# Factorization-machine kernel: the first layer's weights in a transfer of 16 rows, and chunk 0 with the remainder in one

## The reference

```python
x_reg = input_data @ W_lin.T + b_lin                       # 12500 -> 1
emb = input_data @ factors                                 # 12500 -> 16
sum_squared = jnp.square(emb.sum(axis=1))
squared_sum = (jnp.square(input_data) @ jnp.square(factors)).sum(axis=1)
h = jax.nn.relu(emb @ W1.T + b1)                           # 16 -> 128
h = jax.nn.relu(h @ W2.T + b2)                             # 128 -> 64
dnn_out = h @ W3.T + b3                                    # 64 -> 1
x = x_reg + 0.5 * (sum_squared - squared_sum)[:, None] + dnn_out
x = 0.5 + jax.nn.sigmoid(x) * 5.0
```

## Time and profile before

| | |
|---|---|
| median of 3 runs | 133.77 us (133.70 to 133.78) |
| profiled execution | 133.86 us, span 132.0 us |
| TensorE busy | 107.0 us, 81% of the span |
| ScalarE, VectorE, GpSimd busy | 61.4, 52.6, 17.8 us |
| moved by DMA | 52.36 MB, mean 397 GB/s |
| mean granted clock of TensorE | 0.948 |
| chain that ended last | DMA 52%, PE 42%, SyncE's queue 2% |

### The profile page before, as it was taken

One profiled execution on the slowest core, in us unless ns is written; L12 is line 12 of the kernel. 1 busy time (PEld: TensorE's weight loads), 2 busy tenths in 40 slices (PEclk: granted clock), 3 DMA queues, 4 the chain that ended last, 5 costly groups with the idle time before them and its releaser, 6 DMA issues.

```text
span 132.0 us, 2605 instructions
## 1 busy us (share of the span) xinstructions
PE 107.0 (81%) x1123; PEld 34.3 (26%) x1123; DVE 52.6 (40%) x51; ACT 61.4 (47%) x52; POOL 17.8 (14%) x48
## 2 busy tenths in 40 slices
PE   6089569539999749969659979999569997999992
PEld 4012112012222112212112233322022222334881
DVE  0391063037036046045055016564075352576571
ACT  4030067039039049049058046867078472465851
POOL 3015000200046200110200110164200400000000
PEclk9999999965899977999986999999999999999999
DMA  3999899899989999998999999899899999999700
GB/s 115 397 528 427 377 477 452 367 447 477 427 367 477 432 397 437 477 417 387 467 447 397 427 477 417 382 467 437 382 427 432 437 410 422 416 399 413 306 23 1
DMA packets 3345, 52.36 MB, mean 397 GB/s; under 512 B 388, under 2 KB 520, under 8 KB 1544
## 3 DMA queue, kind: packets, MB, share of 16 engines
q1 hardware_dynamic: 3336, 52.23, 93.1%
HBM read 52.22 MB, written 0.00 MB: 396 GB/s over the span
## 4 chain that ended last, share of the span: by engine, by line
DMA 52%; PE 42%; SPq 2%; DVE 1%; issue 1%; ACT 1%
PE p_lin L506 37%; DMA xr<-in_x_pairs 36%; DMA xr<-in_x_end 16%; PE p_h L601 2%; PE p_sq L506 2%; PE p_tot L506 1%; PE p_h L632 1%; SPq L273 1%; DVE h L454 0%; DVE h L449 0%; PE p_tot L614 0%; SPq L267 0%; SPq L266 0%; SPq L265 0%; ACT lin L341 0%
## 5 line engine op out<-in xcount | busy, mean ns | idle before, releaser
L327 ACT ACTIVATE sq<-xr 128x2560 f32<-128x2560 f32 x20 | 45.8, 2331 | 46.6 <-DMA xr<-in_x_pairs 43.7
L427 DVE TENSOR_TENSOR sq<-xr 128x1536 f32<-128x1536 f32 x20 | 34.6, 1765 | 53.4 <-DMA xr<-in_x_pairs 48.8
L506 PE MATMUL p_lin<-xr,wr 128*17 128x512 f32 x320 | 42.3, 673 | 15.6 <-DMA xr<-in_x_pairs 15.6
L506 PE MATMUL p_lin<-sq,wz 128*18 128x512 f32 x320 | 36.5, 592 | 0.0
L506 PEld LDWEIGHTS p_lin<-xr,wr 128*17 128x17 f32 x320 | 9.6, 107 | 46.5 <-issue 39.7
L307 POOL COPY wr<-hd 128x136 f32 (+1 forms) x20 | 9.9, 495 | 77.6 <-PE p_lin L506 77.6
L506 PEld LDWEIGHTS p_lin<-sq,wz 128*18 128x18 f32 x320 | 9.8, 98 | 24.8 <-issue 24.7
L506 PE MATMUL p_lin<-xr,hd 128*17 128x352 f32 (+1 forms) x128 | 10.1, 380 | 1.3 <-DMA xr<-in_x_end 1.3
L437 DVE TENSOR_TENSOR sq<-xr 128x1408 f32<-128x1408 f32 (+3 forms) x6 | 6.6, 1134 | 6.2 <-DMA xr<-in_x_end 6.2
L337 ACT ACTIVATE sq<-xr 128x1408 f32<-128x1408 f32 (+3 forms) x6 | 5.7, 982 | 6.4 <-DMA xr<-in_x_end 6.4
L308 POOL COPY wz<-s_all 128x8 f32 (+1 forms) x20 | 7.0, 350 | 0.0
(11 more groups left out here) (52 smaller groups left out, 39.7 us busy)
## 6 DMA issues: line engine op xcount, KB each, us to landing
xr<-in_x_pairs SPq DMA_DIRECT2D x9, 4096.0 KB, 22.0
xr<-in_x_groups SPq DMA_DIRECT2D x2, 2048.0 KB, 17.7
xr<-in_x_end SPq DMA_DIRECT2D x1, 2112.0 KB, 17.2
xr<-in_x_end SPq DMA_DIRECT2D x3, 640.0 KB, 18.7
xr<-in_x_end SPq DMA_DIRECT2D x1, 1760.0 KB, 21.1
xr<-in_x_end SPq DMA_DIRECT2D x1, 1056.0 KB, 16.3
hd<-in_head SPq DMA_DIRECT2D x1, 952.0 KB, 4.8
xr<-in_x_end SPq DMA_DIRECT2D x1, 704.0 KB, 17.6
```

Source lines behind the costliest of these rows:

```text
L327: nc.scalar.activation(sq[:, ring(s), BY_DVE:CHUNKS, :], xr[:, s, BY_DVE:CHUNKS, :], ACT.Square).then_inc(act_squared, 1)
L427: nc.vector.tensor_tensor(sq[:, ring(s), 0:BY_DVE, :], xr[:, s, 0:BY_DVE, :], xr[:, s, 0:BY_DVE, :], ALU.mult).then_inc(dve_squared, 1)
L506: return nc.tensor.matmul(out, lhsT, rhs, start=False, stop=False, skip_group_check=True)
```

## The change

The first layer's weights leave the head: its rows have 1776 columns instead of 1904. They come in a transfer of their own, `w1_once` into the tile `w1_sel`: 16 rows of 256 columns, of which the first 128 are the weights, and the other 128 four identity matrices of 16 x 16, at columns 0, 32, 64 and 96, with zeros between them. At the end of its first stage TensorE multiplies the one by the other into the bank `p_h1[0]`, which gives the weights in four places with zeros in the other rows, and VectorE copies them from PSUM into the tile `w1`, which `first_layer` now reads. Chunk 0 and the remainder lie side by side in one tile `x_one` and in one array, and come in one transfer with one semaphore. Other functions are unchanged.

```diff
-C_W1 = 0
-C_W2 = C_W1 + H1
+C_W2 = 0
 C_B1 = C_W2 + H2
...
-def fm_kernel(nc, head, x_first, x_rest, x_pairs, x_groups, x_end, out):
+def fm_kernel(nc, head, w1_once, x_first, x_pairs, x_groups, x_end, out):
...
-        xf = sb("xf", [P, B])
-        xl = sb("xl", [P, REST_SETS, REST_COLS])
+        w1_sel = sb("w1_sel", [EMB, H1 + P])
+        w1 = sb("w1", [P, H1])
+        x_one = sb("x_one", [P, B + REST_SETS * REST_COLS])
...
+        xf = x_one[:, 0:B]
+        xl = x_one[:, B:].rearrange("p (c b) -> p c b", b=REST_COLS)
...
             sp.dma_start(hd[:, :], head).then_inc(hd_landed, 16)
-            sp.dma_start(xf[:, :], x_first).then_inc(first_landed, 16)
-            sp.dma_start(xl[:, :, :].rearrange("p c b -> p (c b)"), x_rest).then_inc(rest_landed, 16)
+            sp.dma_start(x_one[:, :], x_first).then_inc(first_landed, 16)
+            sp.dma_start(w1_sel[:, :], w1_once).then_inc(w1_landed, 16)
...
-            dve.wait_ge(rest_landed, 16)
+            dve.wait_ge(first_landed, 16)
             nc.vector.tensor_tensor(sql[:, :, :], xl[:, :, :], xl[:, :, :], ALU.mult).then_inc(rest_squared, 1)
+            dve.wait_ge(w1_done, 1)
+            nc.vector.tensor_copy(w1[:, :], p_h1[0][:, 0:H1]).then_inc(w1_ready, 1)
...
-            pe.wait_ge(rest_landed, 16)
             remainder(LIN, wl, xl)
...
             remainder(WZ, ws[:, ENDS + 1:, :], sql)
+            pe.wait_ge(w1_landed, 16)
+            nc.tensor.matmul(p_h1[0][:, 0:H1], w1_sel[:, H1:H1 + P], w1_sel[:, 0:H1],
+                             start=True, stop=True, skip_group_check=True).then_inc(w1_done, 1)
...
-                    mm = nc.tensor.matmul(bank[32 * t:32 * t + 32, 0:n], pr[:, C_W1 + 32 * t:C_W1 + 32 * t + 32], rhs,
+                    mm = nc.tensor.matmul(bank[32 * t:32 * t + 32, 0:n], w1[:, 32 * t:32 * t + 32], rhs,
                                           start=True, stop=True, skip_group_check=True)
...
+            pe.wait_ge(w1_ready, 1)
             layer1(0)
...
-    x_first = np.ascontiguousarray(xT[:P])
+    x_first = np.concatenate([xT[:P], x_rest], axis=1)
...
+    w1_once = np.zeros((EMB, H1 + P), f32)
+    w1_once[:, :H1] = np.asarray(L0_rec_W1).T
     for t in range(4):
-        params[32 * t:32 * t + EMB, C_W1:C_W1 + H1] = np.asarray(L0_rec_W1).T
+        w1_once[:, H1 + 32 * t:H1 + 32 * t + EMB] = np.eye(EMB, dtype=f32)
```

More of the change, by code:

```diff
@@ L134, in fm_kernel @@
         first_landed = sem("first_landed")
-        rest_landed = sem("rest_landed")
+        w1_landed = sem("w1_landed")
+        w1_done = sem("w1_done")
+        w1_ready = sem("w1_ready")
         x_landed = [sem(f"x_landed{t}") for t in range(SLOTS // TWO)]
@@ L724 @@
     xT = np.asarray(r_input_data).T
-    x_first = np.ascontiguousarray(xT[:P])
     rest = np.zeros((REST_SETS * REST_K, B), f32)
     rest[:REST] = xT[P:P + REST]
-    x_rest = np.ascontiguousarray(rest.reshape(REST_SETS, REST_K, P // REST_K, REST_COLS).transpose(2, 1, 0, 3).reshape(P, -1))
+    x_rest = rest.reshape(REST_SETS, REST_K, P // REST_K, REST_COLS).transpose(2, 1, 0, 3).reshape(P, -1)
+    x_first = np.concatenate([xT[:P], x_rest], axis=1)
     chunks = xT[P + REST:].reshape(ALL - 1, P, B)
@@ L762 @@
     params[:, C_B3] = np.asarray(L0_rec_b3)
-    arrays = {"head": head, "x_first": x_first, "x_rest": x_rest, "x_pairs": x_pairs, "x_groups": x_groups, "x_end": x_end}
+    arrays = {"head": head, "w1_once": w1_once, "x_first": x_first, "x_pairs": x_pairs, "x_groups": x_groups, "x_end": x_end}
     nc = bacc.Bacc("TRN2", target_bir_lowering=False, num_devices=1)
```

## The result

The changed kernel takes **134.24 us** (median of 6 runs, 134.14 to 134.36) against 133.72 for the kernel before in the same session (6 runs, 133.69 to 133.78). The ratio is 1.0036, 95% interval 1.0026 to 1.0046: about 0.5 us slower. Forecast were 133.59, a range of 133.20 to 134.00, and 0.12 for slower. The profiled execution took 134.18, its span 132.4.

The account below looks back on a forecast made before the run. The prediction took the full DMA queue as the bound until the last awaited transfer, then a fixed tail. Bytes 0.11 plus rows 0.07 made 0.18 us less than 133.77: 133.59 us, range 133.20 to 134.00.

Parts of the forecast that it names:

- The bound: Transfers fill the DMA queue until the last awaited piece lands at 115.69 us; the end is that landing plus a tail.
- the price of bytes: Bytes queued ahead of the last awaited landing move the end one for one at 437 GB/s; net 49,152 B, 0.11 us.
- the new product and copy: End of TensorE's first stage: product 0.1 to 0.4 us, then VectorE's copy, done between 16.2 and 16.7, not delaying the end.
- cover of 0.8 us: Least time between the end of product and copy and the first pair's landing, which both engines await next.
- a fixed tail: After the last awaited transfer lands at 115.69 us, the nearly all-TensorE work to the end stays unchanged.
- The second defence: Were the first stage late for the first pair, TensorE's 12.4 us of slack in the buffer ring would absorb it.
- The sum of 0.18 us: Opening transfers: 0.11 us from fewer bytes plus 0.07 from fewer rows, all reaching the end.
- the estimate of 3.5 ns: Skill's fixed overhead per packet, about 3 cycles; eight rows would give 0.03 us, the whole sum 0.14 instead of 0.18.
- Rival 1: Instruction fetches fall otherwise on the last DMA engine: 132.99 to 133.50 (0.25 with all else under 133.50) or 134.19 (0.03).
- Rival 2: The small transfer's 16 rows all go to one DMA engine, delaying later landings: 134.14 us, chance 0.05.
- Rival 3: TensorE's clock is lowered after 115.7 us, where it has no idle time: up to 2.8 us, 136.4, chance 0.04.
- Rival 4: The change does nothing, the slowest DMA engine being as late as before: 133.77 us, chance 0.05.

Follow-up runs that it names:

- e7: Kernel before with 512 columns of zeros (256 KB) more in the head; 134.31 us against 133.73, ratio 1.0043.
- e12: Changed kernel with the copy on ScalarE and the small transfer issued four times in a row; 134.60 us against 133.74, ratio 1.0058.
- e1: Kernel before with one one-column memset more on VectorE in the first stage; 134.20 us against 133.76, ratio 1.0032.
- e2: Changed kernel with the copy of the weights out of PSUM on ScalarE instead of VectorE; 133.68 us against 133.76, ratio 0.9996.
- e9: Changed kernel with one one-column memset more on VectorE, two instructions more than the kernel before; 133.77 us, ratio to the kernel before 0.9997.
- e3: Changed kernel with two one-column memsets more on VectorE, three instructions more than the kernel before; 133.70 us, ratio to the kernel before 0.9994.
- e10: Changed kernel with four one-column memsets more on VectorE, five instructions more than the kernel before; 133.75 us, ratio to the kernel before 0.9998.
- e11: Changed kernel with copy on ScalarE, small transfer issued behind the third pair, product and copy just ahead of the first layer; 133.84 us against 133.74, ratio 1.0006.
- e6: Kernel before with only the small transfer, product and copy (on ScalarE), chunk 0 and remainder still two transfers; 133.84 us against 133.73, ratio 1.0009.
- e5: Kernel before with chunk 0 and remainder merged and the head's 128 weight columns dropped without replacement, result wrong; 133.59 us against 133.73, ratio 0.9993.
- e4: Kernel before with only chunk 0 and the remainder merged into one transfer; 133.66 us against 133.76, ratio 0.9992.

## Why the prediction was wrong

**The bound was read rightly.** The end is the last link's landing plus a tail. e7 confirms the price of bytes (0.58 us for a forecast of 0.60), and e12 that a delay ahead of the first pair reaches the last link whole (0.88 and 0.88).

**The step that failed** is the one on the new product and copy: "Behind the copy on VectorE stand only the squares of the first pair", with a cover of 0.8 us. I priced the copy by its duration and by who waits for it where it stands. There both were right: it ran at 16.27 for 0.29 us and nobody waited. What I put at nothing is that an instruction added to an engine's program also shifts all its later instructions by one, and that VectorE pauses for about 0.45 us at some place of that program. With it goes "plus a fixed tail": the tail depends on where that pause falls. e1 shows it without any other part of the change (+0.44 us), e2 takes it away with all other parts kept (0.9996 against 1.0036, 0.53 us), and e9, e3 and e10 show that more instructions don't cost more. The pause ahead of the copy is 0.42 to 0.45 of the 0.5 us by which the kernel is slower. Nothing in the profile before pointed at the price; the pause itself was there, as 0.44 us between two instructions of 0.32.

**The cover of 0.8 us was luck.** The length of TensorE's first stage was taken from one profile, and it is set by the clock. In each trace the records of the granted clock begin only when it is at its full 2.4 GHz, at 10.15 us before, 10.78 after, 12.35 in e1, 13.29 in e2 and 13.67 in e9. Ahead of that the products run at half the pace: sets of four with 256 columns start 0.41 to 0.43 us apart in e2, and 0.21 apart behind it. In e2 the copy ran at 17.39, just ahead of the first pair at 17.50; in e9 it ran at 17.62, and VectorE began the first pair at 17.92, 0.29 behind ScalarE. The second defence held, that a late start there is absorbed later on: e9 stands at 0.9997. As e1 changes no transfer and has a late rise too, one profile each can't say whether the change moves it.

**The sum of 0.18 us** is right for what the DMA engines save, and too large for what reached the end. The packet records hold the cost of a row, for which the prediction found no row in the trace. A row of the head takes 288 ns before and 269 after; rows of 4 and 3 KB take 159 and 121, together 280, and the merged row of 7 KB 272; a row of 1 KB takes 46. With 8 rows to an engine the head saves 0.15 us and the merge 0.06, and the small transfer costs 0.05: 0.17 in all. The 8 ns saved with each row lie in the prediction's 7 to 14; the estimate of 3.5 ns beside them is too low, and the measurement decides.

At the end less is left. The four variants of the changed kernel without the gap and with its transfers (e2, e3, e9, e10) stand at ratios of 0.9994 to 0.9998: 0.03 to 0.08 us less than before, each with 0.12 us to either side, so 0.18 (a ratio of 0.99865) lies outside the intervals of e9 and e10, at the edge of that of e2 and inside that of e3; e11 is at 1.0006. Term by term: the merge gave 0.10 (0.05 to 0.11 forecast); dropping the columns on top of it gave nothing that can be told from noise at the end (0.15 forecast); the small transfer in place of the columns, without the merge, gave +0.11 instead of -0.10, its interval from 0 to 0.24. A part of it may go in the slower first rows of 32 KB behind the small one (in e6 1.28 us on average instead of 1.21), and a part goes between the first pair and the last link, in e5 too. I name no cause for that: it is 0.1 to 0.2 us, and single profiles of kernels with the same transfers differ by as much.

**The rivals.** Rival 1 (fetches that delay a DMA engine): both pages list 7 such fetches, and nothing shows that they delay an engine more than before; its 134.19 is near the measured time by chance. Its sign, a shift that changes between the first pair and the last link, is there, but e5 shows it without a transfer or product added. Rival 2's 134.14 is chance as well: it falls with e2, which keeps the small transfer and is not slower, and with the packet records, which have one row on each engine. That is what "Why a DMA increments its semaphore by 16 and not by 1" in DMA: Bandwidth & Descriptors of the Trainium skill gives for a 16-row transfer, and the traces agree. Rival 3 did not occur: the stretch after 115.8 ran at 1.00. Rival 4 would have been close to the truth, had the pause not moved.

**Two slips without effect:** the DMA engines were full to the 37th slice and not the 38th, and the bytes ahead of the pairs are 1,800 KB with the change and not 1,848.

**No version clearly beats both.** The best complete ones are e4 (133.66), e2 (133.68) and e3 (133.70), all at least 0.5 us faster than the changed kernel; against the kernel before each interval still reaches 1.

## What to carry to other kernels

An added instruction can have two prices: its own time, and the shift of everything behind it in that engine's program. When a small change makes a kernel slower and every transfer and wait is where it should be, look in the chain of waits for an "issue" gap of some tenths of a microsecond on an engine that has just passed a semaphore; then add one or two idle instructions early on that engine, or move the new one to another engine, and measure again before judging the change. The place of the pause can't be computed from what is shown here, so it has to be tried.

A saving of 0.1% in the opening transfers can be seen at the first landing and still be lost among differences of the same size at the last one; size such a claim with a large dose (e7), and look for the records of single packets, which give the price of a row without any run.

## What the hardware did that I had not expected

- VectorE pauses for 0.45 us at one place of its program. In the eleven kernels with none or one instruction more that is ahead of its 79th recorded instruction: behind the copy (nine kernels, partly covered) or ahead of it (after and e1, in full view). With two, three and five more it isn't seen, and a fetch of instructions comes 8 us earlier.
- A 16-row transfer goes to 16 engines, one row each. Three more of them, issued in a row ahead of the first pair, delay it by 0.88 us, 0.29 each, against 0.04 each by bytes; most of it is in the long rows right behind the short ones, 1.73 us on average instead of 1.21.
- A row of a transfer costs 8 to 9 ns beyond its bytes at 27.3 B per ns: rows of 4 and 3 KB take 159 and 121 ns, one of 7 KB takes 272.
- In the first stage TensorE ran at half its speed, though the table has a granted clock of 1.00 there: 4 matmuls of 512 columns took 3.42 us and then 1.89. The records of the clock begin only at 10.15 us in the kernel before, about where the products become fast, so the table's 1.00 ahead of that rests on no record. They begin between 10.15 and 14.38 us in the traces of this case.
